# A graph network's edge MLP: weights centred once instead of every product, two pairs of gelu tiles, moment products behind the first layer

## The reference, cut to what matters

```python
def layer_norm(x, g, b):
    mu = jnp.mean(x, axis=-1, keepdims=True)
    var = jnp.mean((x - mu) ** 2, axis=-1, keepdims=True)
    return (x - mu) * jax.lax.rsqrt(var + EPS) * g + b
...
d = jax.nn.gelu(layer_norm(x @ Wd1 + bd1, g1, b1), approximate=False)
d = jax.nn.gelu(layer_norm(d @ Wd2 + bd2, g2, b2), approximate=False)
```

## Time and profile before

| what | value |
|---|---|
| median of 3 runs | 3817.49 us (3815.22 to 3842.65) |
| span of the profiled execution | 4406.9 us |
| stage `mg` in it, first product to last gelu | 56.4 to 794.3 us |
| phase 1, phase 2, phase 3 | about 399, 237 and 95 us |
| clock granted to TensorE in phases 1, 2, 3 | 0.74, 0.50, 0.50 |

### The profile page before, as it was taken

The page is one execution under the profiler, slowest core; times in us unless marked ns, Lnnn a source line. Parts: engine busy times, 40 slices in busy tenths (PEclk is TensorE's granted clock), DMA queues, the critical chain, the costliest instruction groups (busy, mean ns, idle before and its releaser), DMA issues. The chain is left out here.

```text
span 4406.9 us, 55601 instructions
## 1 busy us (share of the span) xinstructions
PE 2756.5 (63%) x13712; PEld 1883.0 (43%) x13712; DVE 2532.0 (57%) x4681; ACT 1676.6 (38%) x3862; POOL 2245.3 (51%) x2350
## 2 busy tenths in 40 slices
PE   3566653244544456687775858689879997888100
PEld 3555432122222344566442446456546665555100
DVE  5677322286877533466564766366646564666654
ACT  2344212133333100256453711255545564656211
POOL 3777671566777376200488000355544444555576
PEclk9777555566776676788787867699989998888555
DMA  4676201222222222356322124445444443222111
GB/s 114 174 201 199 90 0 43 51 57 56 69 59 60 49 64 61 80 129 138 98 84 66 53 57 96 98 132 149 131 126 129 120 132 98 84 84 81 46 41 32
DMA packets 770354, 399.85 MB, mean 91 GB/s; under 512 B 531868, under 2 KB 676671, under 8 KB 770256
## 3 DMA queue, kind: packets, MB, share of 16 engines
q1 hardware_dynamic: 706268, 340.57, 29.2%
q0 software_dynamic: 64000, 58.26, 5.2%
HBM read 217.04 MB, written 182.59 MB: 91 GB/s over the span
## 5 line engine op out<-in xcount | busy, mean ns | idle before, releaser
L1221 POOL DMA_INDIRECT g_W<-t,g_cols x400 | 439.3, 1098 | 397.4 <-PE g_pS L2707 155.8
L897 POOL DMA_INDIRECT at_W<-in_x,at_idx x400 | 440.1, 1100 | 179.4 <-issue 117.2
L1221 POOL DMA_INDIRECT ou_W<-t,ou_cols x200 | 207.4, 1037 | 154.9 <-PE ou_pA L3003 84.9
L484 POOL DMA_INDIRECT where<-mg_stage_v,mg_stage_i x200 | 233.7, 1169 | 71.1 <-issue 66.2
L2923 POOL DMA_INDIRECT out<-ou_F,ou_ways x200 | 202.3, 1011 | 112.1 <-DVE ou_F L3189 56.0
L1221 POOL DMA_INDIRECT me_W<-t,me_cols x200 | 205.9, 1030 | 95.0 <-issue 59.4
L499 POOL DMA_INDIRECT mg_stage_v<-where,mg_stage_i x200 | 208.1, 1041 | 71.8 <-issue 62.5
L3239 POOL DMA_INDIRECT de_V<-t,de_cols x200 | 208.5, 1043 | 53.2 <-issue 48.4
L967 PE MATMUL at_pL<-at_XF,w_logit 128*128 128x512 f32 x100 | 81.0, 904 | 216.6 <-ACT at_XF L1013 149.7
L1211 POOL COPY g_cols<-pos 128x8 int32 (+1 forms) x50 | 12.5, 250 | 395.5 <-POOLq L81 395.3
L601 PE MATMUL mg_pXT<-ident,mg_z 128*128 128x128 f32 x388 | 85.4, 361 | 155.6 <-DVE mg_z L762 92.3
(11 more groups left out here) (557 smaller groups left out, 8820.6 us busy)
## 6 DMA issues: line engine op xcount, KB each, us to landing
mg_x<-in_x SPq DMA_DIRECT2D x97, 256.0 KB
x<-mg_z SPq DMA_DIRECT2D x97, 256.0 KB
x1T<-mg_zt SPq DMA_DIRECT2D x97, 256.0 KB
at_V<-mlp SPq DMA_DIRECT2D x100, 128.0 KB
t<-up_X SPq DMA_DIRECT2D x100, 128.0 KB
t<-g_HS SPq DMA_DIRECT2D x50, 256.0 KB
t<-g_HD SPq DMA_DIRECT2D x50, 256.0 KB
g_D<-t SPq DMA_DIRECT2D x50, 256.0 KB
```

The source lines that it names most:

```text
L484: gp.indirect_dma_start(out=k.where, out_offset=bass.IndirectOffsetOnAxis(ap=stage_i[b][:, t:t + 1], axis=0), in_=stage_v[b][:, t:t + 1], ...
L897: gp.indirect_dma_start(out=W[w][b][:, (2 * t + h) * C:(2 * t + h + 1) * C], out_offset=None, in_=a["x"], in_offset=bass.IndirectOffsetOnA ...
L1221: nc.gpsimd.indirect_dma_start(out=slot(w, b, t), out_offset=None, in_=table, in_offset=bass.IndirectOffsetOnAxis(ap=cols[w][:, c:c + 1], ...
```

## The change

Seven edits, all in stage `mg` but for the tile and the load of `bd2`:

- `center_weights` on VectorE takes the row means off Wd1 with its bias (four copies), Wd2 (two copies) and bd2, once, before the first step. `bd2` is now loaded into all 128 partitions.
- `center_edges` no longer reduces and subtracts: for the first layer it is one copy of `pz` to `z`, for the second one addition of `bd2`.
- the bias product of the second layer is gone, and `second_layer` covers both `b`.
- the gelu output has two pairs of tiles, `act[0][b]` for even and `act[1][b]` for odd blocks, with a semaphore pair each for their stores.
- in phase 2 TensorE transposes block j+1 before it multiplies block j.
- in phase 1 TensorE runs `first_layer(j+1)` before `gram(2j+1)`.
- GpSimd no longer waits for the edge attributes.

```diff
-        k.bd2 = k.sb("bd2", [1, CT, C])
+        k.bd2 = k.sb("bd2", [P, CT, C])
...
-                    load(k.bd2[:, n, :], row(a["L0_gnn_bd2"], C))
+                    load(k.bd2[:, n, :], row(a["L0_gnn_bd2"], C).to_broadcast([P, C]))
...
-        act = [g.sb(f"act{b}", [P, CE // 2]) for b in range(2)]
+        act = [[g.sb(f"act{w}{b}", [P, CE // 2]) for b in range(2)] for w in range(2)]
...
-                pool.wait_ge(attr_in, 64)
...
-                with sp.Fori(0, ITERS) as j:
+                def store_edges(j, w):
                     for b in range(2):
                         sp.wait_ge(e["gelu", 2], last_of(j, b))
                         rows = k.mlp[:, bass.ds((2 * j + b) * CE, CE)].rearrange("c (n h e) -> c n h e", h=2, e=P)
                         for h in range(2):
-                            sp.dma_start(rows[:, :, h, :], groups(act[b][C * h:C * h + C, :], CT // 2))\
-                                .then_inc(mlp_out[b], 16)
+                            sp.dma_start(rows[:, :, h, :], groups(act[w][b][C * h:C * h + C, :], CT // 2))\
+                                .then_inc(mlp_out[w][b], 16)
...
-                def second_layer(j, b):
-                    pe.wait_ge(e["gelu", 1], last_of(j, b))
-                    reuse(pe, e["cen", 2], 2 * j)
-                    t.matmul(pz[b][:, :], k.ones[0:1, :], k.bd2[:, :, :].rearrange("a n c -> a (n c)"),
-                             start=True, stop=False, skip_group_check=True)
-                    for n in range(CT // 2):
-                        i = t.matmul(pz[b][:, n * P:n * P + P], act[b][:, n * P:n * P + P], k.wd2[:, :],
-                                     start=False, stop=n == CT // 2 - 1, skip_group_check=True)
-                    i.then_inc(e["prod", 2], 1)
+                def second_layer(j, w):
+                    for b in range(2):
+                        pe.wait_ge(e["gelu", 1], last_of(j, b))
+                        reuse(pe, e["cen", 2], 2 * j)
+                        for n in range(CT // 2):
+                            i = t.matmul(pz[b][:, n * P:n * P + P], act[w][b][:, n * P:n * P + P], k.wd2[:, :],
+                                         start=True, stop=True)
+                        i.then_inc(e["prod", 2], 1)
...
                 pe.wait_ge(attr_in, 64)
+                pe.wait_ge(centered_w, 10)
...
+                def layer_step(j, w):
+                    for b in range(2):
+                        turn(j + 1, b, 1)
+                    second_layer(j, w)
...
                 def center_edges(j, layer):
                     for b in range(2):
                         dve.wait_ge(e["prod", layer], last_of(j, b))
-                        v.tensor_reduce(out=zs[b][:, :], in_=groups(pz[b][:, :], CT), op=ALU.add, axis=AX)\
-                            .then_inc(e["sum", layer], 1)
-                    for b in range(2):
-                        dve.wait_ge(e["sum", layer], last_of(j, b))
-                        v.scalar_tensor_tensor(groups(z[:, bass.ds((2 * j + b) * CT * C, CT * C)], CT),
-                                               over(zs[b][:, :], C), -1.0 / C, groups(pz[b][:, :], CT),
-                                               ALU.mult, ALU.add).then_inc(e["cen", layer], 1)
+                        at = z[:, bass.ds((2 * j + b) * CT * C, CT * C)]
+                        if layer == 1:
+                            v.tensor_copy(at, pz[b][:, :]).then_inc(e["cen", 1], 1)
+                        else:
+                            v.tensor_tensor(at, pz[b][:, :], k.bd2[:, :, :].rearrange("p n c -> p (n c)"), ALU.add)\
+                                .then_inc(e["cen", 2], 1)
...
+                def center_weights():
...
+                    for w, first, rows in parts:
+                        at = rowsum[first:first + rows, 0:1] if rows == 4 else rowsum[first:first + rows, 1:2]
+                        v.scalar_tensor_tensor(w, at.to_broadcast([rows, C]), -1.0 / C, w, ALU.mult, ALU.add)\
+                            .then_inc(centered_w, 1)
...
+                center_weights()
                 step(0, None, 0)
```

More of the change, by code:

```diff
@@ L429, in mlp_and_gram_stage @@
         ones_in = g.sem("ones_in"); passed_dve = g.sem("passed_dve")
-        attr_in = g.sem("attr_in"); mlp_out = g.pair("mlp_out")
+        attr_in = g.sem("attr_in"); mlp_out = [g.pair(f"mlp_out{w}_") for w in range(2)]
         e = {}
         for layer in (1, 2):
-            for n in ("prod", "sum", "cen", "sq", "sumsq", "scaled", "turned", "gelu"):
+            for n in ("prod", "cen", "sq", "sumsq", "scaled", "turned", "gelu"):
                 e[n, layer] = g.sem(f"{n}{layer}")
@@ L700, in _, with layer_step @@
                 s.preload_act_table_set(GELU)
-                for b in range(2):
-                    gelu(0, b, 1)
-                with act_.Fori(0, ITERS - 1) as j:
-                    for b in range(2):
-                        gelu(j + 1, b, 1)
+                def layer_step(j, w):
+                    gelu(j + 1, 1 - w, 1)
                     for b in range(2):
                         square_edges(j, b, 2)
+                gelu(0, 0, 1)
+                layer_step(0, 0)
+                layer_step(1, 1)
+                with act_.Fori(0, ITERS // 2 - 1) as i:
+                    layer_step(2 * i + 2, 0)
+                    layer_step(2 * i + 3, 1)
                 for b in range(2):
@@ L711, in _ @@
                 s.preload_act_table_set(GELU)
-                with act_.Fori(0, ITERS) as j:
-                    for b in range(2):
-                        gelu(j, b, 2)
+                gelu(0, 0, 2)
+                gelu(1, 1, 2)
+                with act_.Fori(0, ITERS // 2 - 1) as i:
+                    gelu(2 * i + 2, 0, 2)
+                    gelu(2 * i + 3, 1, 2)
+                gelu(ITERS - 1, 0, 2)
             @block.vector
@@ L718, in _ @@
                 v = nc.vector
+                def center_weights():
+                    parts = [(k.wd1[32 * n:32 * n + 4, :], 32 * n, 4) for n in range(4)] + \
+                        [(k.wd2[C * h:C * h + C, C * h:C * h + C], C * h, C) for h in range(2)]
+                    for w, first, rows in parts:
+                        at = rowsum[first:first + rows, 0:1] if rows == 4 else rowsum[first:first + rows, 1:2]
+                        v.tensor_reduce(out=at, in_=w, op=ALU.add, axis=AX).then_inc(summed_w, 1)
+                    v.tensor_reduce(out=rowsum[:, 2:2 + CT], in_=k.bd2[:, :, :], op=ALU.add, axis=AX)\
+                        .then_inc(summed_w, 1)
+                    dve.wait_ge(summed_w, 7)
+                    for w, first, rows in parts:
+                        at = rowsum[first:first + rows, 0:1] if rows == 4 else rowsum[first:first + rows, 1:2]
+                        v.scalar_tensor_tensor(w, at.to_broadcast([rows, C]), -1.0 / C, w, ALU.mult, ALU.add)\
+                            .then_inc(centered_w, 1)
+                    for n in range(CT):
+                        v.scalar_tensor_tensor(k.bd2[:, n, :], rowsum[:, 2 + n:3 + n].to_broadcast([P, C]), -1.0 / C,
+                                               k.bd2[:, n, :], ALU.mult, ALU.add).then_inc(centered_w, 1)
+                    dve.wait_ge(centered_w, 10)
                 def center_edges(j, layer):
```

44 lines of the change are left out of this document (25 added, 19 removed).

## The result

The changed kernel takes **3800.06 us** (median of 14 runs, 3775.55 to 3825.41); the kernel before, run beside it, 3829.84 us (14 runs, 3810.95 to 3857.46). The ratio is **0.9919, 95% interval 0.9897 to 0.9942**: 0.8% faster, about 30 us, where 2.1% and 79 us were forecast, and 3800 lies above the range. The gain is inside the 1% that the prediction called no change; 14 runs of each are enough to tell it from none.

A forecast was written before the change was run, and what follows sets the result against it. The prediction took the MLP to end stage `mg`, not GpSimd. 87 + 11 + 8 - 15 = 91 us of the profiled 4406.9, in proportion 79 off the median 3817.5, gave 3738, put as 3740 us; range 3700 to 3795.

The forecast's parts named there:

- What bounds the kernel now: Opening part on stage `mg`: three phases with three limits, and a barrier that waits for the MLP, not GpSimd.
- edits at nothing: Stage `mg` and the `bd2` load: `center_weights`, the `bd2` broadcast and GpSimd's 22 us earlier start were each put at nothing.
- 138.5 us of them: Phase 2: of 89 us of waits without a releaser in the trace, 138.5 were said to lie before the gelu.
- The first rival: End of stage `mg`: GpSimd becomes the bound, gain 45 us at most, 22 if both ended together; 3773 to 3795; chance 0.22.
- phase 1: First layer, 399 us: VectorE's waits and some instructions go, transfers come next, 312 us left; gain 87, range 49 to 111.
- phase 2: Second layer, 237 us: a block takes 5.4 us, not 5.9; gain 11 us, range 0 to 30.
- phase 3: Last gelus and stores, 95 us: a tile every 1.69 us, not 1.84; gain 8 us, range 0 to 30.
- given back: Phase 3: waits without a releaser appear beside GpSimd's reads and cost 0 to 23 us, taken as 15.
- the ring: Phase 2: product, addition, square, sum, scaling, transpose and product again follow in series across engines, 5.4 us a block.
- The rule on copies: New VectorE copies: by a skill rule, 50 copies would hold GpSimd back 21 us; by a trace row, nothing.
- The slower rival: Phase 2: each of 24 blocks meets one more unreleased wait of 5.4 us; 37 us slower, 3850; chance 0.05.
- The rival of the transfers: Phase 1: transfers bind earlier and it stays at 350 us; 58 us gained, in proportion 50, 3767; chance 0.12.

The follow-up runs named there:

- b2: The kernel before, unchanged, profiled on the second chip: 4196.82 us (1 run), where the kernel before took 4247.66 us in the median.
- b3: The kernel before, unchanged, profiled once more to see where its stage ends: 3810.78 us.
- e1: The kernel before with one edit, GpSimd does not wait for the edge attributes: 3805.17 us (6 runs), ratio 0.9904.
- e4: The kernel before without GpSimd's 200 position reads and their copies, all positions set to one value: 3805.63 us (6 runs), ratio 0.9918.
- e3: The kernel after without GpSimd's 200 position reads and their copies, all positions set to one value: 3707.57 us (6 runs), ratio 0.9661.
- e9: The kernel before without the 200 position reads, and with phase 1's moment products issued behind the first-layer products: 3753.03 us (1 run).
- e10: The kernel after without the 200 position reads, and with phase 1's old order (moment products ahead of first-layer products): 3754.89 us (1 run).
- e2: The kernel after with one edit, GpSimd waits for the edge attributes again: 3825.66 us (12 runs), ratio 0.9961.
- e5: The kernel after with GpSimd's indirect DMAs in blocks of 50, not 10, on the second chip: 4481.89 us (6 runs), beside 4247.66 before.

## Why the prediction was wrong, point by point

**The step that failed is in the first part, "What bounds the kernel now": "The barrier behind the stage waits for the MLP and not for GpSimd".** It was read rightly from the earlier trace rows, and it is true of that execution and of b2. In b3, an execution about as long as those that the median is made of, it is false: the last gelu is at 656.4 and GpSimd's last copy at 681.7. From it followed the second failure, in the edits at nothing: GpSimd's 22 us "while the MLP ends last that is worth nothing". They were worth 1.0% in e1, as much as the whole change. The sign that was passed over stands in the prediction itself: a profiled execution 589 us longer than the median. Scaling the sum from 91 to 79 spread those us evenly, while in this stage 108 of them (`at_own` at 798.7 and 690.3) sat in the one chain that ended last.

A second reading there does not hold: "138.5 us of them" can't be a part of 89. The 138.5 are all the idle time of ScalarE that ended so, and part of it would have been idle anyway; what lengthened the phase are the 89.

**The first rival, "GpSimd becomes the bound", is what happened**, by the mechanism and nearly by the price: it gave the MLP's end as 708 and GpSimd's as 685, and 3773 to 3795. In truth the order was already the other way round (656 and 682), so its lower case, "22 if the two ended together", was the measure: 27 us for GpSimd's end, 30 for the kernel. That 3800 lies above even this rival's 3795 comes from the base: its 22 to 45 us were taken off 3817.5, the median of 3 runs, and over 14 runs the kernel before takes 3829.84. Its chance of 0.22 was too small, and its argument against, that GpSimd's pace might be shorter too, could have been answered: the median write of GpSimd is 0.97 us long in the recorded execution and in b3 alike, and its stage ends at 684.7 and 681.7.

**The terms of the sum came out inside their ranges (0 to 23 for what is given back), but they belong to a chain that was not the last.** Undisturbed and without GpSimd's reads (e4 less e3), or from b3 to the kernel after:

| term | forecast | e4 to e3 | b3 to after |
|---|---|---|---|
| phase 1 | 87 (49 to 111) | 68 | 68 |
| phase 2 | 11 (0 to 30) | 23 | 28 |
| phase 3 | 8 (0 to 30) | 10 | 10 |
| given back | -15 | none | none |

That 91 was forecast and the last gelus of e4 and e3 lie 99 us apart is partly luck: phase 1 was taken 19 too high, phase 2 12 too low, and the 15 given back did not come.

Phase 1: the wait of VectorE went, the copy cost 0.74 us a pair, and the transfers came next, as said. From the earlier trace rows the 399 us should have become 312; they became 283, at 261 GB/s and with 73.91 MB, at the floor that the prediction named (288, from 76.04 MB at 264 GB/s). But an ordinary execution starts from 354, so the gain is smaller. The order alone brings nearly all of it (63.5 of 68 us in e9), and the instructions taken off VectorE little. Phase 2: the ring is there, and its block of 5.20 us at clock 0.50 answers to the forecast 5.4, where an undisturbed block of the kernel before takes 5.91; over 24 blocks the difference is 17 us. What was not foreseen, and gives the rest, is the clock: at 0.50 to 0.53 with the bias products (b3, e4, e9), at 0.60 to 0.65 without (e3, e10, after), so part of the phase ran at 2.4 GHz; a block there takes 4.05 us (scaling at 371.87 and 375.92, mean clock 0.84 in 370 to 380 us). Phase 3: 1.69 us a tile forecast, 1.66 to 1.72 measured, against 1.85 in b3; that the gelu's wait for a landing would vanish was wrong. In b3 SyncE issues nine stores in 8.02 us, 1.78 a tile, so its queue was close to setting the pace before.

**Edits at nothing.** `center_weights` costs nothing to be seen: e2 starts the first node reduce at 57.0 us, b3 at 56.0. The 58.4 of the kernel after comes with GpSimd's early start, for e1, without `center_weights`, has 58.7. **The rule on copies.** In the kernel after 200 writes keep GpSimd busy 234.3 us, in e10 236.7; without copies they take 238.6 (b3), 236.4 (e4), 228.7 (e1) and 259.9 (e9). The 21 us for which the prediction drew on the Trainium skill's "SBUF — State Buffer", section "Who interferes with whom", did not appear. That section lets a copy take the shared ports only "when their operands meet the conditions" of another page, a condition that the prediction left out. So the runs show that this copy, which reads PSUM, costs GpSimd nothing; they don't try the section's rule on a copy between two tiles in SBUF. What the prediction read from one row of 2.51 us holds over the whole phase: in the kernel after the 23 writes that stand beside a copy, and not beside the node pass's `tensor_tensor` (L798), take 0.97 us in the mean, as the one at 203.67 does; the 78 beside L798 take 1.47, with 3.05 the longest. In b3 60 writes beside the same instruction (L762) take 1.70 each, so 60 times 0.73, an estimate of 44 us, of GpSimd's stream stands beside it, in the chain that ends the stage. No run was made without it.

**The slower rival** did not come: the ring met no waits on a chip without them. The rival of the transfers had the mechanism (12.8 us of new waits for loads) but not the price, 49 us in the earlier trace rows's frame where 116 came.

## What to carry to other kernels

A profiled execution that is 15% longer than the median is a profile of another situation: before a gain is taken from the engine that ends last in it, ask by how much the runner-up is behind once the unexplained waits are taken out, and put the forecast there. Where two chains meet at a barrier, only the later one's own shift counts: a chain shortened by 98 us and the other's wait deleted gave 30 together, and the deleted wait alone gave 35, the same within their intervals. The quickest way to know is to take the other chain away (e3, e4) rather than to argue about the one that was changed.

## What the runs showed of the hardware

Executions on one of the three chips took 4248 us where the same kernel takes 3840 on the others, with waits that have no releaser in the trace while GpSimd issues indirect DMAs back to back: in e5 up to 45 us on VectorE, 42 on ScalarE and 66 on TensorE. The kernel after with blocks of 50 was 5.5% slower than the kernel before there and 2.2% faster on another chip: a staging size for indirect DMAs can't be chosen by runs on one chip.

On the chips without these waits an indirect DMA of one column costs GpSimd 1.27 us in the median (0.97 and a 0.30 gap, rows of GpSimd above); 400 of them are over 500 us of a stage. Beside a `tensor_tensor` of VectorE with two inputs in SBUF one took 1.47 us in the mean in the kernel after, 1.70 in b3, and up to 3.2; beside a copy out of PSUM 0.97.

With the centred weights, and so without the bias products, TensorE has less to do in phase 2 (63 us of 118 in e10, 134 of 144 in e9) and is granted a higher clock there, 0.60 against 0.51. Which piece of that part raises it was not run: the order of the transposes and the tiles differ as well.
